# Maxima scores of an attention layer from three products of parts, two heads' sets in the two row halves of TensorE

## What is computed

```
x = x + attention(layernorm(x))        # 16 heads of 16, rotary positions, causal softmax, biases
x = x + fp4_mlp(layernorm(x))          # 704 wide, silu(gate) * up, then down
# attention
q, k = rope(split(x @ Wq.T + bq)), rope(split(x @ Wk.T + bk));  v = split(x @ Wv.T + bv)
att = softmax(where(causal, q @ k.T / 4, -inf));  y = att @ v;  return y @ Wo.T + bo
# fp4_mlp: before each product, input and weight are rounded in blocks of 16 to the grid
# 0, .5, 1, 1.5, 2, 3, 4, 6 (times max|block| / 6)
```

## Time and profile before

| | us |
|---|---|
| median of 3 runs | 1302.66 (1300.41 to 1303.75) |
| profiled execution, device time | 1298.29 |
| its span, first to last instruction | 1296.5 |
| TensorE busy | 1219.2 (94%) |
| VectorE busy | 1097.2 (85%) |
| ScalarE busy | 763.1 (59%) |
| GpSimdE busy | 470.5 (36%) |

### The profile page before, as it was taken

The page is one execution under the profiler, slowest core; times in us unless marked ns, Lnnn a source line. Parts: engine busy times, 40 slices in busy tenths (PEclk is TensorE's granted clock), DMA queues, the critical chain, the costliest instruction groups (busy, mean ns, idle before and its releaser), DMA issues.

```text
span 1296.5 us, 40306 instructions
## 1 busy us (share of the span) xinstructions
PE 1219.2 (94%) x16886; PEld 689.7 (53%) x16886; DVE 1097.2 (85%) x2946; ACT 763.1 (59%) x1658; POOL 470.5 (36%) x501
## 2 busy tenths in 40 slices
PE   7679999899999999999999999999999999999867
PEld 6445555455555555555466555545545555554345
DVE  5799998889898999979479989899998999985066
ACT  4346776456564676656655655646565675656721
POOL 2944665553221112131445562332221112023145
PEclk9879999899999999999999999999999999999989
DMA  4734222311001101101023222111011100000000
GB/s 105 177 96 118 72 78 62 92 30 43 16 21 38 31 2 43 27 10 36 14 64 91 67 67 60 35 34 39 11 30 35 35 2 19 2 6 14 13 13 17
DMA packets 63937, 57.28 MB, mean 44 GB/s; under 512 B 17534, under 2 KB 57344, under 8 KB 63744
## 3 DMA queue, kind: packets, MB, share of 16 engines
q1 hardware_dynamic: 60728, 53.62, 15.9%
q10 hardware_dynamic: 3028, 1.09, 0.3%
HBM read 37.51 MB, written 16.78 MB: 42 GB/s over the span
## 4 chain that ended last, share of the span: by engine, by line
PE 70%; DVE 16%; ACT 6%; issue 3%; POOL 2%; DMA 2%; ACTq 1%; SPq 0%; DVEq 0%; POOLq 0%
PE bank L920 14%; PE bank L932 14%; PE bank L875 13%; PE bank L896 12%; PE bank L1044 7%; DVE bank L1279 6%; ACT prob L1177 5%; DVE piece_max L1282 4%; PE bank L991 4%; PE bank L1035 2%; PE bank L999 2%; PE bank L927 1%; DVE piece_max L1279 1%; PE bank L1006 1%; PE bank L901 1%
## 5 line engine op out<-in xcount | busy, mean ns | idle before, releaser
L1177 ACT ACTIVATE prob<-bank 128x512 f32<-128x512 f32 (+3 forms) x1280 | 594.5, 542 | 280.2 <-PE bank L896 172.6
L1282 DVE TENSOR_REDUCE piece_max<-bank 128x1 f32<-128x512 f32 x768 | 488.1, 676 | 7.1 <-PE bank L875 6.1
L896 PE MATMUL bank<-q_mem,k_mem 99*32 99x512 bf16 (+13 forms) x5120 | 383.9, 341 | 10.6 <-DMA q_mem<-max_rows 8.1
L875 PE MATMUL bank<-k_mem,q_mem 96*32 96x512 bf16 (+14 forms) x5120 | 381.5, 344 | 9.3 <-DVE piece_max L1279 5.5
L920 PE MATMUL bank<-prob,V 128*32 128x512 f32 (+3 forms) x2560 | 293.8, 531 | 15.6 <-ACT prob L1177 11.9
L1496 POOL TENSOR_TENSOR c_mem<-c_mem 128x256 f32<-128x256 f32 (+2 forms) x74 | 85.0, 1149 | 420.3 <-DVE c_mem L1370 420.3
L875 PEld LDWEIGHTS bank<-k_mem,q_mem 96*32 96x32 bf16 x5120 | 135.4, 96 | 182.8 <-issue 104.1
L896 PEld LDWEIGHTS bank<-q_mem,k_mem 99*32 99x32 bf16 x5120 | 145.3, 96 | 152.9 <-issue 65.4
L1279 DVE CUSTOM_DVE_ANT_0 bank<-bank,past_keys 128x32 f32<-128x32 f32 (+15 forms) x512 | 207.9, 468 | 2.8 <-PE bank L875 2.5
L920 PEld LDWEIGHTS bank<-prob,V 128*32 128x32 f32 x2560 | 70.6, 110 | 67.3 <-ACT prob L1177 30.0
L901 PE MATMUL bank<-mask_kq,ident_h 128*32 128x128 bf16 (+3 forms) x2048 | 100.7, 200 | 0.0
(11 more groups left out here) (173 smaller groups left out, 1394.5 us busy)
## 6 DMA issues: line engine op xcount, KB each, us to landing
parts_dram<-a_mem SPq DMA_DIRECT2D x13, 512.0 KB, 3.5
q_mem<-parts_dram SPq DMA_DIRECT2D x32, 192.0 KB, 2.9
k_mem<-parts_dram SPq DMA_DIRECT2D x32, 192.0 KB, 3.5
q_mem<-parts_dram SPq DMA_DIRECT2D x32, 128.0 KB, 3.0
k_mem<-parts_dram SPq DMA_DIRECT2D x32, 128.0 KB, 3.5
c_mem<-in_L_attn_x SPq DMA_DIRECT2D x30, 128.0 KB, 2.1
out<-c_mem SPq DMA_DIRECT2D x30, 128.0 KB, 1.7
a_mem<-in_L_attn_x SPq DMA_DIRECT2D x13, 256.0 KB, 2.8
```

The source lines that it names most:

```text
L875: m = pe.matmul(b[COLUMNS * h:COLUMNS * (h + 1), of], q_rows(u)[0:TERM_ROWS, h, block * COLUMNS:(block + 1) * COLUMNS], k_rows(k0 // CHUNK ...
L896: mm = pe.matmul(b[k0:k0 + COLUMNS, since:CHUNK], k_rows(j // TPC, g)[:, h, first:first + COLUMNS], q_rows(u)[:, h, since:CHUNK], start=Tr ...
L1177: act.activation(prob[:, n % NP, off:CHUNK], bank_of("st", n)[:, off:CHUNK], ACT.Exp, scale=SCALE).then_inc(drained("st", n)[0], 1)
L1282: r = dve.tensor_reduce(most, scores, AX.X, ALU.max)
```

## The change

1. **Three products instead of six for the maxima.** The term rows are dealt anew: rows 0 to 47 hold the three largest products (64 to 111 hold the others for the even heads, and rows 48 to 63 are zeros). For odd heads the two halves are swapped, so that their three largest products lie in rows 64 to 111. The maxima use only those 48 rows. The probabilities use rows 0 to 114, all six products, zeros and the three rows of maxima (now rows 112 to 114).
2. **Two sets.** A piece is now 64 queries of the two even heads, in array rows 0 to 63, or of the two odd heads, in rows 64 to 127. Even and odd pieces alternate in the order, each in its own bank. 768 pieces of earlier keys stay; own pieces are 320, ten in each unit.
3. **Masks on TensorE.** An own piece gets, after each block's four matmuls, four of `mask_qk` by `ident_h` (line 948 of the changed kernel), 64 or 32 columns wide. VectorE uses `tensor_reduce` for all pieces (line 1353).
4. **DMAs.** Six for queries and six for keys in each unit, half as large each, and six for the maxima. In chunk 0 the keys are dealt from ScalarE's queue. Five new DMAs of 256 KB write the zero rows.
5. **The plan** knows a third division, by rows, for the maxima; it charges 96 ns for going to it, and takes the two halves as running side by side in full. `S_IN_FLIGHT` and `ST_IN_FLIGHT` go from 3 to 4, `BESIDE_NS` from 2500 to 500 (0 for whole), and the MLP's head starts `c` from (0, -2000) to (1000, 500).

```diff
-RUNS = ((0, 3), (3, 2), (5, 1))
+RUNS = ((64, 0, 3), (0, 64, 2), (32, 96, 1))
+UPPER_ROWS = 3 * HD
+ZERO_ROW, MAX_ROW = 3 * HD, 64 + 3 * HD
-S_IN_FLIGHT, ST_IN_FLIGHT = 3, 3
+S_IN_FLIGHT, ST_IN_FLIGHT = 4, 4
+BESIDE_NS = dict(whole=0, columns=500, rows=500)
...
     def do(self, engine, name, ns, after=(), shares=False, tile=(WHOLE, None)):
+        if engine == "pe":
+            self.engine_free["pe"] = self.tensor_free(tile)
+            if tile[0] != self.division:
+                ns, self.division = ns + (JOIN_NS if tile[0] == WHOLE else DIVIDE_NS), tile[0]
...
+        if engine == "pe" and tile[0] == BY_ROWS:
+            self.engine_free["pe"], self.rows_free[tile[1]] = begin + ISSUE_NS, max(self.rows_free + [begin + ns])
...
-    BLOCKS = CHUNK // COLUMNS
+    BLOCK = 2 * COLUMNS
+    BLOCKS = CHUNK // BLOCK
-        pieces += [(u, [(0, n, j * BANK, BANK, j, False)]) for n in range(BLOCKS) for j in range(c)]
+        pieces += [(u, odd, [(0, n, j * BANK, BANK, j, False)]) for n in range(BLOCKS) for j in range(c) for odd in range(2)]
...
             def maxima():
-                        for h in range(GROUP):
-                            m = pe.matmul(b[COLUMNS * h:COLUMNS * (h + 1), of],
-                                          q_rows(u)[0:TERM_ROWS, h, block * COLUMNS:(block + 1) * COLUMNS],
-                                          k_rows(k0 // CHUNK, g)[0:TERM_ROWS, h, k0 % CHUNK:k0 % CHUNK + keys],
-                                          start=True, stop=True)
+                        for tile in range(GROUP):
+                            at32, head = tile // 2 * COLUMNS, 2 * (tile % 2) + odd
+                            of = keys - COLUMNS + at32 if own else keys
+                            m = pe.matmul(b[COLUMNS * tile:COLUMNS * (tile + 1), column:column + of],
+                                          q_rows(u)[rows, head, block * BLOCK + at32:block * BLOCK + at32 + COLUMNS],
+                                          k_heads(k0 // CHUNK, g)[rows, head, k0 % CHUNK:k0 % CHUNK + of],
+                                          start=True, stop=not own, skip_group_check=own)
+                        for tile in range(GROUP if own else 0):
+                            at32 = tile // 2 * COLUMNS
+                            m = pe.matmul(b[COLUMNS * tile:COLUMNS * (tile + 1), column + keys - BLOCK + at32:column + keys],
+                                          ident_h[half, HALF_ROWS * odd:HALF_ROWS * odd + COLUMNS],
+                                          mask_qk[half, 0:BLOCK - at32], start=False, stop=True, skip_group_check=True)
...
-                            r = dve.tensor_tensor_reduce(scores, scores, past_keys[:, BANK - keys:BANK], scale=1.0, scalar=LOWEST,
-                                                         op0=ALU.add, op1=ALU.max, accum_out=most)
-                        else:
-                            r = dve.tensor_reduce(most, scores, AX.X, ALU.max)
+                        r = dve.tensor_reduce(piece_max[:, u % 2, n_, slot:slot + 1],
+                                              bank_of("s1", n)[:, column:column + keys], AX.X, ALU.max)
```

More of the change, by code:

```diff
@@ L134, in through @@
         self.end[free] = self.bank_free[b]
-        self.do("pe", use, ns, [*after, free], divided=divided)
+        self.do("pe", use, ns, [*after, free], tile=tile)
         self.start(self.drain(use, b, engine, drain_ns, drain_after, first), self.running[1])
@@ L346, in rehearse_key_ones @@
             yield from plan.wait(until=lambda: not spare_users[c])
+            yield from plan.load("sp", ("key zeros", c), 256)
             yield from plan.load("sp", ("key ones", c), 48)
@@ L357, in rehearse_deals, with key_queue @@
             free = stored + ([("st", GROUP * final_step[u - Q_SLOTS] + 3)] if u >= Q_SLOTS else [])
[L358 to L359 removed]
+            for n, (_, _, terms) in enumerate(RUNS):
+                for odd in range(2):
+                    yield from plan.load("sp", ("deal q", u, n, odd), 32 * terms, free)
             free = stored + ([("st", GROUP * final_step[(NCHUNKS - 1) * NGROUPS + g] + 3)] if k >= NCHUNKS else [])
[L361 to L368 removed]
+            for n, (_, _, terms) in enumerate(RUNS):
+                for odd in range(2):
+                    yield from plan.load(key_queue(k), ("deal k", u, n, odd), 32 * terms, free)
+    def key_queue(k):
+        return "act" if k == 0 else "sp"
+    def rehearse_maxima():
+        for n, (u, odd, parts) in enumerate(pieces):
+            keys, own, last = sum(part[3] for part in parts), parts[0][5], (len(RUNS) - 1, 1)
+            yield from plan.wait([("deal q", u, *last), ("q zeros",)]
+                                 + ([("deal k", u, *last), ("masks",), ("key zeros", units[u][0] % NCHUNKS)] if own else [])
+                                 + ([("place", u - 2, 2 * SPLIT - 1)] if u >= 2 else [])
                                  + ([("drain", "s1", n - S_IN_FLIGHT)] if n >= S_IN_FLIGHT else []))
[L370 to L371 removed]
+            yield from plan.through(("s1", n), 0.428 * keys + 20 * len(parts) * own, "dve", 66 * len(parts) + 1.04 * keys, [], [],
+                                    tile=(BY_ROWS, odd))
             if n == final_piece[u]:
@@ L385, in rehearse_placing @@
         free = [("st", GROUP * final_step[u - Q_SLOTS] + 3)] if u >= Q_SLOTS else []
-        for p in range(SPLIT):
-            yield from plan.load("act" if placed_by_scalar(u) else "sp", ("place", u, p), 4, [("neg5", u)] + free)
+        for n in range(2 * SPLIT):
+            yield from plan.load("act" if placed_by_scalar(u) else "sp", ("place", u, n), 2, [("neg5", u)] + free)
     def rehearse_probabilities():
@@ L673, in preln_layer @@
         q_dealt = [sem(f"q_slot{s}_dealt") for s in range(Q_SLOTS)]
+        first_k_dealt = [sem(f"k_group{g}_first_dealt") for g in range(NGROUPS)]
         k_dealt = [sem(f"k_group{g}_dealt") for g in range(NGROUPS)]
@@ L1268, in maxima @@
             def maxima():
-                for n, (u, parts) in enumerate(pieces):
+                for n, (u, odd, parts) in enumerate(pieces):
                     yield when["drain", "s1", n]
```

244 lines of the change are left out of this document (133 added, 111 removed).

## The result

The changed kernel takes **1337.0 us** (median of 4 runs, 1334.4 to 1339.1) where the kernel before takes 1303.2 beside it: the ratio is 1.024, interval 1.021 to 1.027. It is slower by 34 us; the forecast said 1332. The profiled execution spans 1333.9 us against 1296.5, 37.4 more, and what follows divides up those 37.4.

The account below looks back on a forecast made before the run. TensorE was taken as the bound, VectorE close to its limit. Maxima -38.1, changes +66.6, waits -8, start +5, placing +4 make +29.5 on 1298.3: 1327.8; the median lies 4.4 higher, so 1332 us, 8-in-10 range 1271 to 1366.

Parts of the forecast that it names:

- Own pieces: Maxima of a unit's own keys, masks included: 2.44 us a unit instead of 1.85, 18.9 us more for 32 units.
- the start: Before the first probabilities: 24 key DMAs on ScalarE's queue and 1.3 MB of zeros cost 5 us, bounds 0 and 15.
- the waits: TensorE's waits for VectorE: of 24.2 us, 8 go as VectorE gets about 14 us less work; bounds 0 and 24.
- the clock: No term; if the clock were granted at half from 81 us on, the time would be above the range.
- the price of a change: Each change of TensorE's array division costs 0.092 us; 724 more of them add 66.6 us.
- The ends of the runs: At the end of each of 424 runs of maxima the second half ends about 0.03 us later: 12.7 us.
- Maxima of earlier keys: 320 pairs run beside each other in the row halves, 128 pieces have no partner: 57.0 us gained on TensorE.
- the two halves don't overlap here, as I read it: matmuls start in program order: In own pieces, the odd piece stands behind the even piece's masks, which wait for that piece's columns.
- Rival C: The two row halves run free of each other's order and own pieces overlap: 38 us off, 1294; chance 0.05.
- Placing: DMAs that place the maxima, six instead of three: 1.8 us later in each unit, 4 us in all, bounds 0 and 20.
- The eleven waits: Probabilities' waits for placing DMAs in the kernel before, 18.6 us together; eleven times 1.8 gave the upper bound 20.
- The 20 to 35 us: Expected rise of the waits for `q_mem<-max_rows`, the placing of the maxima, to 20 to 35 us.

Follow-up runs that it names:

- run 1: Kernel before, maxima from three of six products in rows 0 to 47, dividing the rows with nothing beside them: 1447.2 us, ratio 1.108.
- run 4: Changed kernel, zeros read from a constant of 16 distinct rows instead of one 512-byte row over and over: 1331.7 us, ratio 1.019.
- Run 9: Changed kernel, planner's `BESIDE_NS` for columns and rows 2000 instead of 500, giving 896 changes of division instead of 1046: 1387.9 us, ratio 1.063.
- run 3: Changed kernel, masks of own pieces moved ahead of their columns in the order: 1339.4 us, ratio 1.025.

## Why the prediction was right, and where it was not

The direction, the size and the mechanism of the two main terms hold. Own pieces, the start, the waits and the clock were wrong, the price of a change was read too low, and the errors nearly cancelled.

- **The price of a change (+66.6 us): right in mechanism, read about 0.015 us too low.** That changes between rows and columns cost as much as the others was taken without a row that shows it, and holds: run 1 and the medians say so. The size is off because two distances were compared that begin at different matmuls. In the earlier trace rows the 0.31 us start at the last of a bank's four matmuls (the row has x1), the 0.22 of the earlier trace rows at the first. From first to first the medians at full clock are 0.326 us from a full bank of maxima to probabilities and 0.327 the other way, against 0.216 without a change; the kernel before has 0.32 from a full bank to the whole array. Behind whole-array matmuls the price is the 0.092 that was said. A second part stands in the earlier trace rows and was not counted: from 1123.64 to 1124.61 there are 0.97 us for four matmuls that otherwise start 0.216 apart. In both traces the first two whole-array matmuls of 256 columns after a change start 0.320 us apart, 0.10 more. By these medians and the counts of each kind the added changes are about 86 us. The ends of the runs, for which the prediction had 12.7, are then about 4. Together this is an estimate of 11 us more than was said. The rule it cited from the Trainium skill (TensorEngine Tiling (Array Packing), Key Properties), that changing the mode drains TensorE, agrees with these rows: each kind of change has its 0.09 to 0.11 us.
- **Maxima of earlier keys (-57.0): right.** One pair takes 0.34 us and two take 0.56, change included: about 0.218 each. Of the 0.122 left, which the prediction splits into 0.03 for the end and 0.092 for the change, 0.11 is the change.
- **Own pieces (+18.9): wrong in sign.** The failed step is "the two halves don't overlap here, as I read it: matmuls start in program order". A unit takes 1.5 to 1.7 us, less than the 1.85 before, so the term is -5 to -12. Rival C had the mechanism right with a chance of 0.05, and the time wrong (1294). The prediction read from four column tiles within one row range what two row halves would do. It also leaned on a sentence of the Trainium skill (TensorE: Matmul & The Clock Gate, Part 3), that matmuls start and end in program order in different tiles too; the rows at 1060.26 to 1060.44 show starts of another order across row halves, and the measurement decides. The rows of the kernel before at 1122.80 and 1122.81 could have warned it.
- **VectorE's waits (-8): not seen.** VectorE is less busy by 8 us (1089 instead of 1097; 1083 was said), but weight loads wait for it longer (46.7 instead of 37.2 us; the 24.2 of the prediction left out two rows), and matmuls as long as before (5.8 and 5.5). As TensorE's idle time after 92 us is the same in both kernels, the term is about 0.
- **Start (+5): too small.** The first probabilities start 14.4 us later instead of within 5. Up to there TensorE is idle for 10.9 us more and busy for 3.4 more, with 502 matmuls instead of 332 and partly at half clock; I count 12 of the 14.4 as the start. The prediction counted ScalarE's queue and the bytes of the zeros; what decided was the form of the zeros' transfer (run 4).
- **Placing (+4): 0 here**, all but the one wait at the start. The eleven waits that the prediction counted were no eleven: six of weight loads and five of matmuls are largely the same ones. The 20 to 35 us that it wanted to see hold only in this double count (11.7 + 10.2), for one wait. Run 9 shows that the term was near.
- **The clock: no term.** It was only named as something that would refute the forecast. Half clock costs 10.5 us more than before, 8 of them after 92 us, where the kernel before lost 6 (its 1.00 in the earlier trace rows is rounded: it had half clock from 247 to 254 us).

With the terms mended but the prediction's price of a change the 37.4 us are: changes +67, earlier keys -57, own pieces about -9, start +12, half clock after the start +8. That leaves some 16 us. They lie in TensorE's busy time, not in its idle time: busy time at full clock grew by 15.7, of which the first three terms make 1. The price of a change as the medians give it, with the ends of the runs, accounts for about 11 of the 16. It is an estimate from medians, and no run was made for it. What the other 5 or so are **stays open**; waits too short to show as idle time are a candidate that nothing here isolates.

That measured and forecast time agree to 5 us is therefore partly luck: own pieces were priced 28 us too high and placing 4, while the start was 7 us too low, the clock 8, the waits 8 and the changes about 11.

## What to carry to other kernels

Dividing the array's rows pays per bank saved and costs per change of division: here a pair saves 0.22 us and a run costs two changes, 0.20 to 0.22, so a run must hold two pairs before it is worth anything, and the work beside it must tolerate such runs. Count the changes in the final order before counting the saved banks. And an order in which every wait is hidden is a result of its own: moving one constant of its planner cost 47 to 146 us, more than the whole change, so a new variant is to be compared in its own best order.

## What the runs showed of the hardware

- Matmuls in the two row halves start out of program order with each other: an odd piece's 352 columns at 1060.34, ahead of the even piece's masks at 1060.44 that stand before it in the program. Moving those masks changed nothing (run 3: 1339.4 us beside 1337.0).
- A change of division costs 0.09 us behind whole-array matmuls and 0.10 to 0.11 behind matmuls on 32 columns, with rows divided or not (0.326 us from bank to bank instead of 0.216). Into the whole array it costs once more: the first two matmuls of 256 columns start 0.320 us apart, later ones 0.216.
- Filling 16 rows of 16 KB by reading one 512-byte row again and again takes 8.1 to 13.7 us to land, from distinct rows 4.5 to 6.1, and transfers issued right behind the former were late too (9 us instead of 2 to 3; 4.3 to 5.4 behind the latter).
- After a stretch with a wait of 3 us (busy 0.87 of 4) TensorE's clock was granted at 0.50 in the next, then 0.90 and 1.00 (run 9); in the changed kernel it is 1.00 from 231 to 658 us. So a wait can cost more than its length. A wait of 2.4 us in the kernel before was followed by 1.00.
